# Early-fusion block on one core: the gated product of the expert layer goes from VectorE to ScalarE and GpSimd, and two expert units change stage

## The chip, the cores and the metric

The kernel runs on one core of a Trainium2 chip. A core has five engines that each run their own program: TensorE (PE in the profile, its weight loads PEld), VectorE (DVE), ScalarE (ACT), GpSimd (POOL) and SyncE (SP, which here issues the DMAs). They wait for each other only by semaphores. The metric is the device time of one execution in microseconds (us).

## The reference, cut to what matters

For each of 8 images an attention-free token mixer makes a hidden state `h` of 256 rows, 128 text embedding rows are put under it (T = 384 rows of 256), then comes attention with relative positions over 16 heads, then a dense mixture of 8 experts, which is where the change is:

```
weights = routing_weights(x, Wr, temperature)          # [T, 8], x = layernorm(h)
gate = einsum('btd,edi->beti', x, Wg)                  # all 8 experts, for all rows
up   = einsum('btd,edi->beti', x, Wu)
h    = silu(gate) * up                                 # the gated product
out  = einsum('bte,betd->btd', weights, einsum('beti,eid->betd', h, Wd))
```

## The kernel before, in words

**Rounds.** `rounds` (line 420) lays out one list of named steps per image and every engine walks the same list, doing its own part of each step (or nothing). Image `b` has the stages mix (`mix_in` to `project_v`), maxima (24 items), negate, attend (24 items) and out (`turn_outputs` to `rel_values`). The expert layer (FFN) of image `b-1` is cut into 48 units, and these are placed between the attention steps of image `b`. So there are 8 rounds with attention, of which 7 (b = 1 to 7) also carry the units of the image before, and a tail in which the last image's units run alone.

**Units.** Each expert `e` has two hidden tiles, n = 2e and 2e+1, of 128 hidden rows by T = 384 columns. `gate n` and `up n` are six fp32r matmuls each, into PSUM banks G and U (`hidden_tile`, matmul at L913). `down e 0` and `down e 1` are eight and four matmuls (L934). In the text g9 is gate 9, u9 up 9, d4.0 down 4 part 0. The order is g0 u0 g1 u1, then for each e: g(2e+2) u(2e+2) d(e).0 d(e).1 g(2e+3) u(2e+3).

**After each up.** ScalarE puts `silu(G)` into the single buffer `silu` (L1070); VectorE multiplies it with U into one of three slots of `hT` (L1362). A step after a unit is "late": `fill` holds it back and places it just ahead of the next unit, so behind every attention step that lies between. G may be written again when silu is done, U when the product is done (`h_done`), `silu` may be written again when the product is done; `down e 0` waits for the products of its two tiles. After each down VectorE adds the weighted result to `res` (L1374), which frees the PSUM banks D.

**Placement.** `FILL_MIX`, `FILL_MAXIMA`, `FILL_NEGATE` and `FILL_OUT` say how many units follow each step. Before: 26 units in mix, 8 in maxima (after items 2, 5, 8, ...), 3 in negate, 11 in out.

**Mix.** VectorE makes statistics of two tiles, GpSimd the root (L1405, L1408), VectorE normalises (L1115), GpSimd multiplies by `ln_g` (L1439) and adds `ln_b` (L1441), two tiles each; then statistics of three tiles, GpSimd's root again, VectorE's norm, and TensorE turns the result (L658, `turn_norm`) and projects. VectorE's routing steps lie in between. The projections q and k are each split in three bf16 parts (L1197, L1199, L1201), go through DRAM by SP's queue (L561, L566), and after them the relative logits come back as `band_t` (L595). ScalarE copies the logits out as bf16 at L1002.

**Maxima.** Item n is two score tiles in two of four banks. TensorE may write item n when VectorE has reduced item n-2 (L1220). The first item needs VectorE's copy of `band_t` (L1214). ScalarE re-orders further heads of the band (L1011). At item 13 `negate 0` turns the maxima found so far into bank 5, which is one of D's banks: TensorE first waits until VectorE has added the last down issued so far (`seen["down"]`).

**Out.** ScalarE copies the turned attention (L1047) and the turned weights (L1042); TensorE's `rel_values` (L874) and `residual` (L884) follow. SP writes and reads bands through DRAM (L631, L640).

Of the kernel before, what the change touches and what calls it, by code (L numbers as in the profile page):

```python
# [28 lines left out]
ALU = mybir.AluOpType  # L29
ACT = mybir.ActivationFunctionType  # L30
AX = mybir.AxisListType.X

P = 128
# [5 lines left out]
T = L + TXT  # L39
TT = T // P  # L40
IT = L // P
AH, AD = 16, 16
WIN = 4
NJ = 2 * WIN + 1
NE = 8
FI = 256
FT = FI // P
# [25 lines left out]
WINS = P // BL  # L73
# [6 lines left out]
FILL_MIX = [("residual", 0), ("mix_in", 0), ("turn_x2", 0), ("mix_sums", 0), ("router", 1),  # L80
            ("mix_out", 0), ("router_zone", 1), ("mix_norm", 1), ("router_rank", 2),
            ("norm_stats", 2), ("router_pick", 1), ("turn_norm", 2), ("project_qk", 0),
            ("project_rel", 1), ("project_v", 15)]
FILL_MAXIMA = [0, 0, 1] * 8
WEIGHTS_MAXIMA, WEIGHTS_ATTEND = (10, 18), (2, 12)
VALUE_TILES = (2, 0, 1)
FILL_NEGATE = 3
# [18 lines left out]
def fusion_block(nc, a, out):  # L106
    ctx = ExitStack()

    def sb(name, shape, dt=F32):
        return ctx.enter_context(nc.sbuf_tensor(name, shape, dt))  # L110
# [4 lines left out]
    def sem(name):  # L115
        return ctx.enter_context(nc.semaphore(name))

    def sig(name, n, unit=1, first=0):
        return Signal(sem(name), n, unit, first)

    with ctx:
# [24 lines left out]
        wu_hi = sb("wu_hi", [P, NE, KT, FI], F32R)  # L146
        wu_lo = sb("wu_lo", [P, NE, KT, FI], F32R)
# [19 lines left out]
        x2_hi = sb("x2_hi", [P, KT, T], F32R)  # L167
        x2_lo = sb("x2_lo", [P, KT, T], F32R)
        wgt = sb("wgt", [P, TT, NE])
        silu = sb("silu", [P, T])  # L170
        hT = sb("hT", [P, 3, T])
        stat = sb("stat", [P, TT, 6])
        mv = sb("mv", [P, TT, 2])
# [58 lines left out]
        O, G, U = S[:, 3], S[:, 6], S[:, 7]  # L232
# [56 lines left out]
        win_done = sig("win_done", WINS * AH // 2)  # L289
# [16 lines left out]
        R_STEPS = 24  # L306
        r_dve = sig("r_dve", R_STEPS)
        gate_pe, up_pe = sig("gate_pe", NE * FT), sig("up_pe", NE * FT)
        silu_done = sig("silu_done", NE * FT)
        h_done = sig("h_done", NE * FT)  # L310
        down_pe = sig("down_pe", 2 * NE)
        acc_done = sig("acc_done", NE * TT, first=1)
# [19 lines left out]
        def schedule(attention, ffn, more=True):  # L332
# [11 lines left out]
            def fill(n):  # L344
                for _ in range(min(n, len(left))):
                    unit = left.pop(0)
                    flush()
                    if owed and unit[0] == "down" and unit[2]:
                        steps.append(owed.pop())
                    steps.append(unit)  # L350
                    if unit[0] in after:
                        late.append((after[unit[0]],) + unit[1:])
                        seen[unit[0]] += 1
# [16 lines left out]
            for n in range(ITEMS):  # L370
                steps.append(("maxima", n))
                if not ffn and n in WEIGHTS_MAXIMA:
                    steps.append(("more_weights", WEIGHTS_MAXIMA.index(n)))
                fill(FILL_MAXIMA[n])
                if n == ITEMS // 2 + 1:
# [43 lines left out]
        def rounds(engine, parts):  # L419


            def do(step, b, f):
                part = parts.get(step[0])
                if part is not None:
                    part(f if step[0] in LATE_STEPS else b, *step[1:])

            for s in schedule(True, False):
                do(s, 0, None)
            with engine.Fori(1, NB - 1) as b:
                for s in schedule(True, True):  # L430
                    do(s, b, b - 1)
            for s in schedule(True, True, False):
                do(s, NB - 1, NB - 2)
            for s in schedule(False, True):
                do(s, None, NB - 1)
# [220 lines left out]
        def _(pe):  # L656
# [248 lines left out]
            def hidden_tile(f, n, dst, hi, lo, done, free):  # L905
                e, m = n // FT, n % FT

                if n:
                    pe.wait_ge(free.sem, free.at(f, n))
                j = 0  # L910
                for ws, xs in ((hi, x2_hi), (hi, x2_lo), (lo, x2_hi)):
                    for k in range(KT):
                        mm = pe.matmul(dst[:, 0:T], ws[:, e, k, m * P:(m + 1) * P], xs[:, k, :],  # L913
                                       start=(j == 0), stop=(j == 3 * KT - 1))
                        j += 1
                mm.then_inc(done.sem, 1)
# [2 lines left out]
                hidden_tile(f, n, G, wg_hi, wg_lo, gate_pe, silu_done)  # L919

            def up(f, n):
                hidden_tile(f, n, U, wu_hi, wu_lo, up_pe, h_done)

            def down(f, e, part):
                if part == 0:
# [6 lines left out]
                for i in ((0, 1), (2,))[part]:  # L932
                    for m in range(FT):
# [9 lines left out]
                        "turn_outputs": turn_outputs, "rel_values": rel_values, "turn_attn": turn_attn,  # L943
                        "residual": residual, "turn_x2": turn_x2, "router": router, "gate": gate,
                        "up": up, "down": down})


        @block.scalar
        def _(act):
# [116 lines left out]
            def gate(f, n):  # L1066
                act.wait_ge(gate_pe.sem, gate_pe.at(f, n + 1))
                if n:
                    act.wait_ge(h_done.sem, h_done.at(f, n))
                nc.scalar.activation(silu[:], G[:, 0:T], ACT.Silu).then_inc(silu_done.sem, 1)  # L1070

            rounds(act, {"mix_in": mix_in, "prepare": prepare, "turn_norm": turn_norm,
                         "project_qk": project_qk, "project_rel": project_rel, "maxima": maxima,
                         "negate": negate, "attend": attend, "copy": copy, "turn_weights": turn_weights,
                         "turn_attn": turn_attn, "turn_x2": turn_x2, "router": router, "gate": gate})


        @block.vector
        def _(dve):
# [131 lines left out]
            def maxima(b, n):  # L1211
                if n == 0:
                    dve.wait_ge(band_t_in.sem, band_t_in.at(b, 1))
                    dve.tensor_copy(band_h[:, :, 0:2], band_t[:, :, :, 0:2].rearrange("p i w h -> p i h w")  # L1214
                                    ).then_inc(band_first.sem, 1)
                dve.wait_ge(max_pe.sem, max_pe.at(b, n + 1))
                (h, i), (h2, _) = tiles_of(n)
                dst = maxima_sb[:, i, h:h + 2] if h2 > h else maxima_sb[:, 0:2, h]
                c0 = 2 * (n % 2)
                dve.tensor_reduce(dst, S[:, c0:c0 + 2, PAD:PAD + T], AX, ALU.max).then_inc(max_done.sem, 1)  # L1220
# [132 lines left out]
                step(dve.tensor_tensor(wgt[:], w, each(rt[8][:, :, 1]), ALU.mult))  # L1353
                assert k[0] == R_STEPS

            def hidden(f, n):
                dve.wait_ge(silu_done.sem, silu_done.at(f, n + 1))
                dve.wait_ge(up_pe.sem, up_pe.at(f, n + 1))
                if n >= 3:

                    dve.wait_ge(down_pe.sem, down_pe.at(f, 2 * ((n - 3) // FT + 1)))
                dve.tensor_tensor(hT[:, n % 3], silu[:], U[:, 0:T], ALU.mult).then_inc(h_done.sem, 1)  # L1362

            def accumulate(f, e, part):
                dve.wait_ge(down_pe.sem, down_pe.at(f, 2 * e + part + 1))
                if e and part == 0:
                    dve.wait_ge(acc_done.sem, acc_done.at(f, TT * e))
                last = e == NE - 1
                if last and part == 0 and not (isinstance(f, int) and f == NB - 1):

                    dve.wait_ge(win_done.sem, win_done.at(f + 1, WINS * 6))
                    dve.wait_ge(pv_done.sem, pv_done.at(f + 1, AH // GRP))
                for i in ((0, 1), (2,))[part]:
                    dve.scalar_tensor_tensor((out_st if last else res)[:, i], D[:, i // 2, (i % 2) * E:(i % 2 + 1) * E],  # L1374
                                             wgt[:, i, e:e + 1], res[:, i], ALU.mult, ALU.add
                                             ).then_inc(acc_done.sem, 1)
# [5 lines left out]
                         "turn_weights": turn_weights, "rel_values": rel_values, "residual": residual,  # L1382
                         "turn_x2": turn_x2, "router": router, "router_zone": router_zone,
                         "router_rank": router_rank, "router_pick": router_pick,
                         "hidden": hidden, "accumulate": accumulate})


        @block.gpsimd
        def _(pool):
# [12 lines left out]
            def root(b, stats, steps, done, tiles):  # L1402

                pool.wait_ge(stats.sem, stats.at(b, steps))
                nc.gpsimd.tensor_tensor(rstd[:, 0:tiles], mv[:, 0:tiles, 1], eps[:].broadcast_to([P, tiles]),  # L1405
                                        ALU.add).then_inc(done.sem, 1)
                pool.wait_ge(done.sem, done.at(b, 1))
                nc.gpsimd.tensor_tensor(rstd[:, 0:tiles], rstd[:, 0:tiles],  # L1408
                                        neg_half[:].broadcast_to([P, tiles]), ALU.pow
                                        ).then_inc(done.sem, 1)  # L1410
# [85 lines left out]
            def residual(b):  # L1496
                root(b, ln3, 2 * TT, ln3_root, TT)

            rounds(pool, {"mix_in": mix_in, "mix_sums": mix_sums, "mix_out": mix_out,
                          "mix_norm": mix_norm, "norm_stats": norm_stats, "project_rel": project_rel,  # L1500
                          "weights": weights, "attend": attend, "residual": residual})


# [36 lines left out]
```

## Time and profile before

| what | value |
|---|---|
| median of 3 runs | 1249.13 us (1246.06 to 1252.84) |
| profiled execution, own time | 1249.12 us |
| its span, first to last instruction | 1247.3 us, mean granted TensorE clock 0.952 |
| busy PE / DVE / ACT / POOL | 82% / 60% / 36% / 20% |

A timeline row gives the start, the length of the merged stretch, engine, line, operation, output and inputs, a count, and in square brackets how long the engine had been idle before it and what ended that. A stretch of x3 has three instructions. A row of groups gives the count, the busy time in us and the mean of one in ns, then the idle time before. A granted clock of 1.00 is 2.4 GHz and 0.50 is 1.2 GHz. A round is 143.37 us long in the middle of the run; the image-3 round's maxima stage starts at 518 us, and the image-4 round's mix stage lies about 595 to 661 us.

### The profile page before, as it was taken

What the parts mean: (1) busy time and instruction counts of PE and PEld (TensorE: products, weight loads), DVE (VectorE), ACT (ScalarE), POOL (GpSimd) and SP (SyncE); (2) the same over time, 40 slices, a digit from 0 to 9 for tenths busy, and PEclk for the clock granted to TensorE, in tenths of its full rate; (3) what the DMA queues carried; (4) which work ended last, traced back from release to release, by engine and by line L of the source; (5) the groups of instructions that cost most, each with busy time, mean ns of one, the idle gap of its engine ahead of it and who ended that gap; (6) DMA issues with size and microseconds to landing.
All of it is one profiled execution on the core that took longest, in us unless ns stands there. A gap on an engine that the chain in (4) does not pass through costs nothing.

```text
span 1247.3 us, 16776 instructions
## 1 busy us (share of the span) xinstructions
PE 1020.4 (82%) x5668; PEld 744.4 (60%) x5668; DVE 753.0 (60%) x1597; ACT 451.2 (36%) x651; POOL 247.8 (20%) x262
## 2 busy tenths in 40 slices
PE   3536698888898798888898798988988888987798
PEld 2412277636786287745786377854876367862687
DVE  7347355774648755685658745685567746487343
ACT  1133512453124723355124622346224531347211
POOL 6228411021200402013200412004120212004000
PEclk9569789989999999999999999999999999999899
DMA  4286203602062110802044020722026020620100
GB/s 110 101 240 174 68 5 97 140 11 53 4 178 59 24 42 33 202 10 39 18 121 115 9 56 0 202 44 39 18 79 157 10 52 5 179 60 18 35 1 13
DMA packets 96962, 87.87 MB, mean 70 GB/s; under 512 B 67281, under 2 KB 85074, under 8 KB 95090
## 3 DMA queue, kind: packets, MB, share of 16 engines
q1 hardware_dynamic: 96524, 86.24, 28.3%
q0 software_dynamic: 384, 1.05, 0.3%
q8 instruction: 17, 0.28, 0.1%
q14 instruction: 37, 0.30, 0.1%
HBM read 60.35 MB, written 26.92 MB: 70 GB/s over the span
## 4 chain that ended last, share of the span: by engine, by line
PE 46%; issue 22%; DVE 17%; DMA 5%; ACT 4%; POOL 4%; SPq 2%; POOLq 0%; DVEq 0%; ACTq 0%
PE S L913 16%; PE S L934 8%; DVE maxima L1220 4%; PE S L844 4%; PE S L779 4%; PE S L827 4%; PE S L741 3%; DVE S L1241 3%; ACT scratch L1033 3%; PE S L658 1%; DMA txt_row<-in_L_txt_W_E,txt_idx 1%; DVE res L1374 1%; PE S L760 1%; SPq L566 1%; PE S L787 1%
## 5 line engine op out<-in xcount | busy, mean ns | idle before, releaser
L1491 POOL TENSOR_TENSOR bands<-scratch,one 64x432 f32<-64x432 f32 x128 | 119.1, 931 | 525.0 <-ACT scratch L1033 519.4
L1070 ACT ACTIVATE silu<-S 128x384 f32<-128x384 f32 x128 | 63.0, 492 | 352.2 <-PE S L913 243.6
L1220 DVE TENSOR_REDUCE maxima<-S 128x2 f32<-128x768 f32 x192 | 172.2, 951 | 19.0 <-PE S L787 17.6
L934 PE MATMUL S<-w_d,hT 128*128 128x256 f32 x768 | 182.0, 382 | 1.5 <-DVE hT L1362 0.7
L1241 DVE TENSOR_TENSOR S<-S,bands 64x144 f32<-64x144 f32 x384 | 154.3, 402 | 43.3 <-PE S L827 32.6
L1033 ACT ACTIVATE scratch<-S 128x768 f32<-128x768 f32 x192 | 154.8, 812 | 56.3 <-DVE S L1241 43.0
L779 PE MATMUL S<-k_st,q_st 128*128 128x384 bf16 x384 | 101.9, 334 | 68.0 <-DVE maxima L1220 39.7
L934 PEld LDWEIGHTS S<-w_d,hT 128*128 128x128 f32 x768 | 143.4, 191 | 22.2 <-issue 2.3
L1362 DVE TENSOR_TENSOR hT<-silu,S 128x384 f32<-128x384 f32 x128 | 70.7, 552 | 116.7 <-PE S L913 97.4
L827 PE MATMUL S<-q_st,k_st 128*128 128x384 bf16 x384 | 98.8, 356 | 40.2 <-ACT scratch L1033 36.7
L1011 ACT ACTIVATE scratch<-scratch 128x816 bf16<-128x816 bf16 x56 | 92.3, 1694 | 41.5 <-DMA scratch<-d_band_t 41.5
L779 PEld LDWEIGHTS S<-k_st,q_st 128*128 128x128 bf16 x384 | 37.6, 98 | 116.3 <-DVE maxima L1220 58.0
L1374 DVE SCALAR_TENSOR_TENSOR res<-S,wgt,res 128x256 f32<-128x256 f32 x168 | 75.5, 479 | 48.0 <-PE S L934 47.7
L827 PEld LDWEIGHTS S<-q_st,k_st 128*128 128x128 bf16 x384 | 25.6, 99 | 132.1 <-ACT scratch L1033 104.0
L844 PE MATMUL S<-scratch,v_one 128*17 128x384 f32 x768 | 84.0, 522 | 12.4 <-ACT scratch L1033 12.3
L913 PE MATMUL S<-x_hi,wu_hi 128*128 128x384 f32 x256 | 72.1, 363 | 23.7 <-DVE hT L1362 23.7
L787 PE MATMUL S<-scratch,ident_b 128*128 128x132 bf16 (+1 forms) x384 | 85.7, 224 | 0.0
L913 PE MATMUL S<-x_hi,wg_hi 128*128 128x384 f32 x256 | 78.1, 386 | 0.0
L658 PE MATMUL S<-ident,scratch 128*128 128x128 f32 (+1 forms) x196 | 30.2, 294 | 51.5 <-DVE scratch L1115 29.9
L913 PE MATMUL S<-x_lo,wu_hi 128*128 128x384 f32 x256 | 66.4, 341 | 0.0
L913 PE MATMUL S<-x_hi,wg_lo 128*128 128x384 f32 x256 | 66.4, 341 | 0.0
L913 PE MATMUL S<-x_lo,wg_hi 128*128 128x384 f32 x256 | 66.3, 340 | 0.0
(167 smaller groups left out, 1515.6 us busy)
## 6 DMA issues: line engine op xcount, KB each, us to landing
bands<-d_band_s SPq DMA_DIRECT2D x16, 864.0 KB, 9.4
scratch<-d_band_t SPq DMA_DIRECT2D x8, 1632.0 KB, 9.6
d_parts<-scratch SPq DMA_DIRECT2D x48, 192.0 KB, 1.9
q_st<-d_parts SPq DMA_DIRECT2D x48, 192.0 KB
k_st<-d_parts SPq DMA_DIRECT2D x48, 192.0 KB
d_band_w<-bands SPq DMA_DIRECT2D x32, 240.0 KB, 3.9
out<-scratch SPq DMA_DIRECT2D x8, 384.0 KB, 2.6
x_in<-in_x SPq DMA_DIRECT2D x8, 256.0 KB, 3.6
```

Source lines behind the costliest of these rows:

```text
L779: pe.matmul(S[:, bank, PAD:PAD + T], q_st[:, h, i * P:(i + 1) * P], k_st[:, h, :], start=True, stop=False, skip_group_check=True)
L787: mm = pe.matmul(S[rows, bank, at + w0:at + w1], ident_b[rows, rows], band_h[rows, i, h, w0:w1], start=False, stop=True, skip_group_check= ...
L827: mm = pe.matmul(S[:, 2 * (n % 3) + l, PAD:PAD + T], k_st[:, h, i * P:(i + 1) * P], q_st[:, h, :], start=True, stop=True)
L844: mm = pe.matmul(S[32 * l:32 * l + VC, 6 + g % 2, 0:T], v_one[:, i, h, :], p_t[:, h % PTS, i, :], start=(i == VALUE_TILES[0]), stop=(i == ...
L913: mm = pe.matmul(dst[:, 0:T], ws[:, e, k, m * P:(m + 1) * P], xs[:, k, :], start=(j == 0), stop=(j == 3 * KT - 1))
L934: mm = pe.matmul(D[:, i // 2, (i % 2) * E:(i % 2 + 1) * E], hT[:, (FT * e + m) % 3, i * P:(i + 1) * P], w_d[:, e, m, :], start=(m == 0), s ...
L1011: nc.scalar.activation(band_h[:, :, heads], band_t[:, :, :, heads].rearrange("p i w h -> p i h w"), ACT.Copy).then_inc(band_turned.sem, 1)
L1033: nc.scalar.activation(dst, S[:, c0:c0 + 2, PAD:PAD + T], ACT.Exp).then_inc(exp_done.sem, 1)
L1220: dve.tensor_reduce(dst, S[:, c0:c0 + 2, PAD:PAD + T], AX, ALU.max).then_inc(max_done.sem, 1)
L1241: dve.tensor_tensor(win, win, band, ALU.add).then_inc(sc_add.sem, 1)
L1374: dve.scalar_tensor_tensor((out_st if last else res)[:, i], D[:, i // 2, (i % 2) * E:(i % 2 + 1) * E], wgt[:, i, e:e + 1], res[:, i], ALU. ...
L1491: nc.gpsimd.tensor_tensor(bands[rows, :, :, 2 * pair:2 * pair + 2].rearrange("p i w h -> p h i w"), win, one[rows].unsqueeze(2).unsqueeze( ...
```

## The change

The product leaves VectorE. ScalarE copies U into a new buffer `up_sb`; GpSimd multiplies `silu` by `up_sb` into `hT`. U is free after the copy (`up_copied`) and no longer after the product. `silu` and `up_sb` are single buffers, so silu n+1 and copy n+1 wait for product n on GpSimd. `project_v` is followed by 13 units for 15, and maxima has 10 units for 8: after items 1, 4, 5, 7, 10, 11, 13, 16, 17, 19. The units that change stage are d3.0 and d3.1, and every unit behind them up to u11 takes another place among the items.

```
-            ("project_rel", 1), ("project_v", 15)]
-FILL_MAXIMA = [0, 0, 1] * 8
+            ("project_rel", 1), ("project_v", 13)]
+FILL_MAXIMA = [0, 1, 0, 0, 1, 1] * 3 + [0, 1, 0, 0, 0, 0]
...
-        silu = sb("silu", [P, T])
+        silu, up_sb = sb("silu", [P, T]), sb("up_sb", [P, T])
...
             def up(f, n):
-                hidden_tile(f, n, U, wu_hi, wu_lo, up_pe, h_done)
+                hidden_tile(f, n, U, wu_hi, wu_lo, up_pe, up_copied)
...
+            def hidden(f, n):                       # ScalarE
+                act.wait_ge(up_pe.sem, up_pe.at(f, n + 1))
+                if n:
+                    act.wait_ge(h_done.sem, h_done.at(f, n))
+                nc.scalar.activation(up_sb[:], U[:, 0:T], ACT.Copy).then_inc(up_copied.sem, 1)
...
-            def hidden(f, n):                       # VectorE
-                dve.wait_ge(silu_done.sem, silu_done.at(f, n + 1))
-                dve.wait_ge(up_pe.sem, up_pe.at(f, n + 1))
-                if n >= 3:
-                    dve.wait_ge(down_pe.sem, down_pe.at(f, 2 * ((n - 3) // FT + 1)))
-                dve.tensor_tensor(hT[:, n % 3], silu[:], U[:, 0:T], ALU.mult).then_inc(h_done.sem, 1)
...
+            def turn_outputs(b):                    # GpSimd
+                pool.wait_ge(win_done.sem, win_done.at(b, WINS * AH // 2))
+
+            def hidden(f, n):                       # GpSimd
+                pool.wait_ge(silu_done.sem, silu_done.at(f, n + 1))
+                pool.wait_ge(up_copied.sem, up_copied.at(f, n + 1))
+                if n >= 3:
+                    pool.wait_ge(down_pe.sem, down_pe.at(f, 2 * ((n - 3) // FT + 1)))
+                nc.gpsimd.tensor_tensor(hT[:, n % 3], silu[:], up_sb[:], ALU.mult).then_inc(h_done.sem, 1)
```

## Rows read from the trace of the kernel before

**Rows 1.** The page: TensorE's busy time, and the ended-last chain by engine.

```profile
PE 1020.4 (82%) x5668; PEld 744.4 (60%) x5668; DVE 753.0 (60%) x1597; ACT 451.2 (36%) x651; POOL 247.8 (20%) x262
PE 46%; issue 22%; DVE 17%; DMA 5%; ACT 4%; POOL 4%; SPq 2%; POOLq 0%; DVEq 0%; ACTq 0%
```

**Rows 2.** Groups by line: busy us, mean ns of one, idle before.

```profile
L1362 DVE TENSOR_TENSOR hT<-silu,S 128x384 f32<-128x384 f32 x128 | 70.7, 552 | 116.7 <-PE S L913 97.4 <-ACT silu L1070 15.5 <-DVE scratch L1335 1.1
L1070 ACT ACTIVATE silu<-S 128x384 f32<-128x384 f32 x128 | 63.0, 492 | 352.2 <-PE S L913 243.6 <-DVE hT L1362 108.6
L1451 POOL TENSOR_TENSOR hid<-hid,bo_all 128x768 f32<-128x768 f32 x8 | 14.8, 1846 | 25.5 <-DVE scratch L1115 25.5
L1439 POOL TENSOR_TENSOR hid<-hid,ln_g 128x256 f32<-128x256 f32 x16 | 12.5, 784 | 7.0 <-DVE hid L1115 7.0
```

**Rows 3.** Timeline of the image-4 mix stage, by engine.

```profile
619.82 0.62 PE L913 MATMUL S<-x_hi,wu_hi 128*128 128x384 f32 x2 [1.54 <-DVE hT L1362]
621.53 0.73 POOL L1441 TENSOR_TENSOR hid<-hid,ln_b 128x256 f32<-128x256 f32 x1
623.67 0.62 PE L913 MATMUL S<-x_hi,wu_hi 128*128 128x384 f32 x2 [1.48 <-DVE hT L1362]
624.84 2.75 PE L934 MATMUL S<-w_d,hT 128*128 128x256 f32 x12
627.75 0.88 DVE L1374 SCALAR_TENSOR_TENSOR res<-S,wgt,res 128x256 f32<-128x256 f32 x2
629.64 0.87 PE L658 MATMUL S<-ident,scratch 128*128 128x128 f32 x6 [2.06 <-DVE scratch L1115]
```

**Rows 4.** Timeline of the image-3 round, end of mix and first maxima item.

```profile
496.49 0.56 ACT L1002 ACTIVATE scratch<-scratch 128x432 bf16<-128x432 f32 x1
497.62 0.96 DVE L1201 TENSOR_TENSOR scratch<-scratch 128x768 bf16<-128x768 f32 x1
514.04 2.75 PE L934 MATMUL S<-w_d,hT 128*128 128x256 f32 x12
516.78 1.67 ACT L1011 ACTIVATE scratch<-scratch 128x816 bf16<-128x816 bf16 x1 [3.10 <-DMA scratch<-d_band_t]
517.97 0.34 PE L779 MATMUL S<-k_st,q_st 128*128 128x384 bf16 x1 [1.18 <-DVE scratch L1214]
```

**Rows 5.** One line's instructions: shortest, median and longest ns.

```profile
L1332 DVE TENSOR_TENSOR scratch<-scratch,earlier x8: 358/784/787, 186.5 to 1187.5; 128x192 f32<-128x192 f32 x8
```

**Rows 6.** Image-3 maxima stage: timeline rows of PE and DVE.

```profile
519.64 0.34 PE L779 MATMUL S<-k_st,q_st 128*128 128x384 bf16 x1 [0.61 <-DVE maxima L1220]
520.06 0.59 PE L913 MATMUL S<-x_hi,wg_hi 128*128 128x384 f32 x2
521.20 0.34 PE L779 MATMUL S<-k_st,q_st 128*128 128x384 bf16 x1
525.08 2.69 DVE L1220 TENSOR_REDUCE maxima<-S 128x2 f32<-128x768 f32 x3 [0.54 <-PE S L787]
544.95 0.49 PE L658 MATMUL S<-ident,maxima 128*8 128x128 f32 x3 [0.19 <-DVE maxima L1220]
```

**Rows 7.** The same stage in the chain that ended last: start, us.

```profile
533.17 1.78 PE S L934 x8
```

**Rows 8.** Image-3 out stage, timeline of three engines.

```profile
589.17 0.86 ACT L1042 ACTIVATE scratch<-S 72x384 f32<-72x384 f32 x2 [0.89 <-PE S L658]
589.59 1.99 PE L934 MATMUL S<-w_d,hT 128*128 128x256 f32 x8
```

**Rows 9.** Window 1193 to 1197: length, busy us of PE, PEld, DVE, ACT, POOL, granted clock, DMA.

```profile
1193.00:1197.00 4.00, 4.00 (x16) 3.44 (x15) 1.08 (x3) 0.00 (x0) 0.00 (x0) 0.70 0.00 0
```

**Rows 10.** The tail's timeline, TensorE.

```profile
1191.78 0.82 PE L913 MATMUL S<-x_hi,wu_hi 128*128 128x384 f32 x2 [2.60 <-DVE hT L1362]
1193.68 3.62 PE L934 MATMUL S<-w_d,hT 128*128 128x256 f32 x12
1240.96 2.86 PE L934 MATMUL S<-w_d,hT 128*128 128x256 f32 x12 [0.70 <-DVE hT L1362]
```

More of the change, by code:

```diff
@@ L308, in fusion_block @@
         gate_pe, up_pe = sig("gate_pe", NE * FT), sig("up_pe", NE * FT)
-        silu_done = sig("silu_done", NE * FT)
+        silu_done, up_copied = sig("silu_done", NE * FT), sig("up_copied", NE * FT)
         h_done = sig("h_done", NE * FT)
@@ L1074, in _ @@
                          "negate": negate, "attend": attend, "copy": copy, "turn_weights": turn_weights,
-                         "turn_attn": turn_attn, "turn_x2": turn_x2, "router": router, "gate": gate})
+                         "turn_attn": turn_attn, "turn_x2": turn_x2, "router": router, "gate": gate, "hidden": hidden})
         @block.vector
@@ L1384, in _ @@
                          "router_rank": router_rank, "router_pick": router_pick,
-                         "hidden": hidden, "accumulate": accumulate})
+                         "accumulate": accumulate})
         @block.gpsimd
@@ L1497, in residual @@
                 root(b, ln3, 2 * TT, ln3_root, TT)
+            def turn_outputs(b):
[6 more added lines that the diff above has]
+                nc.gpsimd.tensor_tensor(hT[:, n % 3], silu[:], up_sb[:], ALU.mult).then_inc(h_done.sem, 1)
             rounds(pool, {"mix_in": mix_in, "mix_sums": mix_sums, "mix_out": mix_out,
                           "mix_norm": mix_norm, "norm_stats": norm_stats, "project_rel": project_rel,
-                          "weights": weights, "attend": attend, "residual": residual})
+                          "weights": weights, "attend": attend, "turn_outputs": turn_outputs, "residual": residual,
+                          "hidden": hidden})
 _NAMES = ["x", "L0_tok_w_bias", "L0_tok_Wk_b", "L0_tok_Wv_b", "L0_tok_Wq_b", "L0_tok_out_w", "L0_tok_out_b",
```

## The prediction, made before the changed kernel was run

> **What bounds the kernel now.** I read the page first. TensorE is busy 82% of the span and holds 46% of the chain that ended last, VectorE 17%, GpSimd 4% [rows 1]. So neither a lighter VectorE nor a heavier GpSimd says anything by its share; what counts is where TensorE waits. The groups by line say what the edit touches: 128 products of 552 ns on VectorE [rows 2]. The timelines then show where those lie. Where units follow each other TensorE never waits for a product. It waits in three places of each round:
>
> - Start of mix: 1.54 and 1.48 us for products, then 2.06 us for VectorE's norm, which comes behind the adds of d0.0 [rows 3].
> - End of mix: the twelve matmuls of d3.0 and d3.1, the two units that are to move, run from 514.04 to 516.79, and TensorE then waits 1.18 us for the band copy. ScalarE, which needs the same transfer, starts at 516.78 on the DMA itself [rows 4]. So the transfer ends this stage, not the units.
> - Maxima: VectorE's reductions (2.69 us for three, 0.87 us each to the next) are the clock of the stage, with a hole of 0.54 us for each gate or up put in [rows 6].
>
> **Durations of the new pieces.** Copy of U on ScalarE: like silu, also 128x384 out of PSUM, 0.49 us [rows 2]. Product on GpSimd: no row has its shape. 128x256 with two SBUF inputs takes 0.78 us, 128x768 takes 1.85 us [rows 2]; between them at the same slope it is 1.05 us. The bounds are those two rows; I take 1.05. A semaphore costs about 0.05 us between engines. So from the end of `up` to a usable product it is 0.49 + 1.05 + 0.1 = 1.64 us for 0.6 before.
>
> **Steady units (end of mix, tail): 0.** A pair of tiles takes TensorE 4.2 us. If u(2e+1) is readable at X, its product is there at X + 1.64, and d(e).0 is issued at X + 1.85 (the next gate and up, 2.11, less 0.26 of matmul drain). The cover is 0.2 us, so from a GpSimd product of about 1.25 us on each expert would stall. Silu of the next tile waits for the product and runs X + 1.6 to X + 2.1, again just in time. 63 us less on ScalarE's free time and 71 us less on VectorE buy nothing here.
>
> **Start of mix: +0.3 us a round.** By the order of steps product 0 stands on GpSimd behind the four `ln_g`/`ln_b` operations, which end at 622.26 [rows 3]. Product 0: 622.3 to 623.36. Silu 1 waits for it (single buffer): to 623.9. u1 runs early now (U is free after the copy: it need not wait until 619.82), but g2 waits for silu 1: 623.95. Then u2 at 625.0 and d0.0 at 626.05 (product 1 is ready at about 625.5). Its eight matmuls end at 627.83, the adds start at 628.03 where they started at 627.75 [rows 3], and norm and turn follow them. So the two old waits are gone (3.0 us) and in their place stands one wait of about 4.5 us, from 619.2 to 623.95. GpSimd's root for the next norm stands behind product 1, until 626.6, and is covered by the adds. Bounds: -0.5 (GpSimd quick) to +1.2 (product 1.85).
>
> **End of mix: +0.5 us a round.** Product 3 meets the split of k. Copy 3 comes behind L1002, which ends at 497.05, so the product wants to start at 497.6; VectorE's L1201, with both inputs in SBUF, starts at 497.62 [rows 4]. L1332 shows what such a meeting costs: 784 ns median where GpSimd works, 358 ns in the tail where it does not [rows 5]. If GpSimd is first, L1201, the DMAs queued behind it on SP (the last part, 12 stack transfers, `band_t`) and the end of the stage are 1.05 us later; if VectorE is first, nothing is lost. I take the middle, 0.5. The Trainium skill ("SBUF — State Buffer", "Who interferes with whom") says that a VectorE instruction with two SBUF inputs contends with a GpSimd instruction that reads SBUF, and that the one that issues second blocks until the first is done. The trace agrees for L1332; the rule speaks against this change, since the old product had one input in PSUM.
>
> Two units (1.78 + about 0.85 us) leave this stage, and that is worth 0, as the transfer ends it [rows 4]: TensorE only waits longer, 3.8 us for 1.2.
>
> **Maxima: +2.8 us a round.** I stepped the new order through with the row durations: item 0.42 us of issue (519.64 to 520.06), reducible 0.65 after its start; gate or up 1.14 us (520.06 to 521.20) [rows 6]; down 1.78 [rows 7] and 0.92; reduction 0.87 to the next and item n allowed after reduction n-2. For the old order this gives 26.75 us from item 0 to the last `negate`; the trace has 26.98 (517.97 to 544.95) [rows 4, 6]. For the new order it gives 29.55. VectorE's idle time inside grows from 2.1 to 5.0 us: 0.90 at d3.0 after item 1; 0.61 and 0.70 where g10 and u10 follow items 10 and 11 with no item between; and at d4.0 after item 13 0.47 waiting for the down and 1.21 for the turned maxima. The last is the change of order: `seen["down"]` is now 9, not 8, at `negate 0`, so the turn waits for the adds of d4.0 and VectorE for turn and ScalarE's copy. Its own work falls by only 0.1 (three products out, d3.0's adds in). Bounds: +1.5 (the negate pause half hidden) to +4.
>
> **Out: +2.3 us a round.** Product 15 is "late", so on ScalarE copy 15 stands behind `turn_weights`. Those two copies end at 590.03 [rows 8]. Copy 13 stood behind L1047 in the same way and held u14 by 0.2, so: 590.23, copy to 590.72, product to 591.82, and d7.0 at 591.87 instead of 589.59 [rows 8]. TensorE has nothing ahead of it, and all that follows to the next mix hangs on it. Bounds +1.5 and +3.1. If the copy stood ahead of `turn_weights` it would be 0.8.
>
> **Attend and negate: 0.** Copy 12 and product 12 end near 549.2, before GpSimd's first window.
>
> **TensorE's clock: +2.4 us a round.** In the tail TensorE waits 2.60 us until 1191.78 [rows 10]; the window 1193 to 1197 was granted 0.70, so part of it at the 1.2 GHz level [rows 9]. u2 took 1.90 us there and the twelve matmuls of d0 3.62 [rows 10], against 1.17 and 2.75 at 2.4 GHz [rows 3]: 1.6 us lost. The waits of 1.54, 1.48 and 2.06 us cost nothing. The change makes two waits over 2.6 us in each round, 4.5 at the start of mix and 3.8 before maxima, and what runs after each lies on the path (g2, u2, d0.0; items 0, 1 and d3.0). Bounds 0 and 1.6 each; I take 1.2, near the row, since the order leaves part of the slow stretch beside VectorE.
>
> **Tail: -3.0 us once.** Product 1 stood behind VectorE's routing; now u2 needs only copy 1, and g2, u2, d0 run on: -2.6 for the wait and -1.5 for its clock, together -4.1, of which 0.1 comes back as silu 1 waits for product 0: -4.0. At the end d7.0 waited 0.70 us [rows 10] and waits 1.04 more.
>
> **Sum.** 7 x (0.3 + 0.5 + 2.8 + 2.3) = 41.3; clock 7 x 2.4 = 16.8; tail -3.0: +55.1 on 1249.12 of the profiled execution, which is the median of the runs (1249.13). Forecast 1304.
>
> **Rivals.**
> - A, no clock falls. For it: waits up to 2.06 us cost nothing. Against: 2.60 did. 1249.1 + 41.3 - 3.0 = 1287.
> - B, the clock falls in two more places, at d7.0 (wait 2.3 to 2.4 us) and around `negate 0` (waits 1.1 and 1.4 us). 7 x 2 x 1.4 more: 1324.
> - C, only the maxima order costs; the waits at d7.0 and splits are covered by something I don't see. 7 x 2.8 - 3.0: 1266.
> - D, not slower: the end of mix hangs on TensorE's units after all. In rows 4 the band copy comes within 0.3 us of the last adds, so a transfer that has really landed by 514.2 would let the stage end 2.6 us sooner, and VectorE's 3 x 0.46 us of products would leave the norm chain too. 7 x -4.0 - 3.0: 1218. It decides only if the landing comes 2.6 us before ScalarE's start at 516.78, which ScalarE, idle for 3.10 us on that DMA, speaks against.
>
> **Chances.** Forecast 0.42, A 0.28, B 0.15, C 0.07, D 0.03, else 0.05. Range 1268 to 1326: from near C to just over B. A measurement of this kernel can tell about 0.5% from no change. Faster 0.04 (D and a bit), same 0.02, slower 0.94.
>
> **What would show it.** In the after trace: d7.0 with 2 to 2.5 us idle before it, released by GpSimd; g2 of mix waiting 4 to 5 us for silu; ScalarE's first L1011 again released by DMA, at the same distance from `turn_norm` or 1 us later with L1201 near 1.9 us; maxima 29 to 32 us long with a hole over 1 us before VectorE's `negate 0`; GpSimd's product 1.0 to 1.1 us; clock 0.5 after two waits. Wrong if: the product takes over 1.25 us (steady experts stall, some 8 x 8 times), or the stage starts sooner after the turn.

## The result, and the profile after

The changed kernel takes 1332.92 us (median of 4 runs, 1330.2 to 1335.99), the kernel before 1249.32 us: ratio 1.0662, 95% interval 1.0628 to 1.0696. The forecast was 1304 with a range to 1326. The direction was right; the loss is 84 us (81 between the two profiled executions) where 55 were forecast.

From the page of the changed kernel: busy time, chain by engine, and three groups. L1506 is the product on GpSimd, L1076 the copy on ScalarE.

```profile
PE 1060.1 (80%) x5668; PEld 776.8 (58%) x5668; DVE 698.5 (53%) x1469; ACT 507.0 (38%) x779; POOL 374.5 (28%) x390
PE 45%; issue 17%; DVE 12%; DMA 9%; POOL 5%; ACT 5%; SPq 5%; POOLq 0%; ACTq 0%; DVEq 0%
L1506 POOL TENSOR_TENSOR hT<-silu,up_sb 128x384 f32<-128x384 f32 x128 | 128.8, 1006 | 566.3 <-ACT up_sb L1076 539.0
L1070 ACT ACTIVATE silu<-S 128x384 f32<-128x384 f32 x128 | 62.9, 492 | 296.3 <-PE S L913 204.5
L1076 ACT ACTIVATE up_sb<-S 128x384 f32<-128x384 f32 x128 | 62.4, 488 | 66.3 <-PE S L913 66.3
```

The product takes 1.01 us (1.05 was taken), the copy 0.49. What does not fit is the first number: TensorE does the same 5668 matmuls and is busy 1060 us, for 1020 before [rows 1]. Work that was not added takes 40 us more, so the clock must be looked at. Its mean over the span is 0.919, for 0.952.

I then divided the round of image 4 by TensorE's first row of each stage, in both timelines (us):

| stage | before | after | added | forecast, without clock |
|---|---|---|---|---|
| mix_in to the turn (L658) | 32.18 | 35.15 | 2.97 | 0.3 |
| turn to first maxima item | 31.67 | 32.52 | 0.85 | 0.5 |
| maxima, to `negate 1` | 27.05 | 32.59 | 5.54 | 2.8 |
| `negate 1` to attend | 4.16 | 5.70 | 1.54 | 0 |
| attend | 27.73 | 27.86 | 0.13 | 0 |
| out, to `rel_values` (L874) | 14.57 | 16.97 | 2.40 | 2.3 |
| rest of the round | 6.04 | 6.05 | 0.01 | 0 |
| round | 143.40 | 156.84 | 13.44 | 5.9 |

Where the clock plays no part (out, turn to item) the terms hold to 0.1 and 0.35 us. Start of mix in the timeline of TensorE and GpSimd, to be held against [rows 3]:

```profile
652.09 1.11 POOL L1506 TENSOR_TENSOR hT<-silu,up_sb 128x384 f32<-128x384 f32 x1
653.84 1.01 PE L913 MATMUL S<-x_hi,wg_hi 128*128 128x384 f32 x2 [4.43 <-ACT silu L1070]
657.84 3.77 PE L934 MATMUL S<-w_d,hT 128*128 128x256 f32 x12
662.68 0.88 PE L658 MATMUL S<-ident,scratch 128*128 128x128 f32 x6 [1.07 <-DVE scratch L1121]
```

The two waits of 1.5 us are gone and one of 4.43 us stands in their place, as forecast. But d0's twelve matmuls then take 3.77 us, for 2.75. The maxima stage, TensorE and VectorE, against [rows 4, 6 and 7]:

```profile
695.20 0.50 PE L779 MATMUL S<-k_st,q_st 128*128 128x384 bf16 x1 [4.56 <-DVE scratch L1220]
696.89 3.72 PE L934 MATMUL S<-w_d,hT 128*128 128x256 f32 x8
701.27 2.69 DVE L1226 TENSOR_REDUCE maxima<-S 128x2 f32<-128x768 f32 x3 [3.17 <-PE S L787]
714.90 0.88 DVE L1372 SCALAR_TENSOR_TENSOR res<-S,wgt,res 128x256 f32<-128x256 f32 x2 [0.40 <-PE S L934]
715.83 0.49 PE L658 MATMUL S<-ident,maxima 128*8 128x128 f32 x3 [0.97 <-DVE res L1372]
716.96 0.55 DVE L1231 SCALAR_TENSOR_TENSOR neg_max<-S,neg_max 8x384 bf16<-8x384 f32 x1 [1.18 <-ACT neg_max L1020]
728.04 0.89 PE L913 MATMUL S<-x_hi,wg_hi 128*128 128x384 f32 x2
```

The first wait is 4.56 us (forecast 3.8 plus the split's delay). d3.0 takes 3.72 us for its eight matmuls, where d4.0 had 1.78 [rows 7], and VectorE's hole behind it is 3.17 us, not 0.90. VectorE's two pauses at `negate 0` are 0.40 us, for the down, and 1.18 us, for the turned maxima; 0.47 and 1.21 were worked out. TensorE's turn waits 0.97 us for the adds of d4.0. In the last row g12's first pair takes 0.89 us for 0.60: slow again, a third place. Windows over the three places give the granted clock; the columns are length, busy time and count of PE, PEld, DVE, ACT, POOL, then the clock:

```profile
653.50:660.00 6.50, 6.16 (x18) 5.75 (x19) 3.00 (x17) 1.65 (x4) 3.01 (x4) 0.51 0.00 0
695.00:701.00 6.00, 5.80 (x19) 4.01 (x20) 1.96 (x3) 2.64 (x3) 1.00 (x1) 0.51 0.53 115
728.00:732.00 4.00, 4.00 (x17) 3.96 (x15) 0.55 (x1) 1.00 (x3) 0.00 (x0) 0.57 0.02 6
```

These are 1.2 GHz for nearly all of 16.5 us. The round before had one slow stretch, 3.4 us within 697.0 to 700.6, some 4.5 us into attend; the changed kernel has that one too (738.2 to 741.8), so the three are new. The split of k, VectorE and GpSimd, against [rows 4]:

```profile
673.98 1.00 POOL L1506 TENSOR_TENSOR hT<-silu,up_sb 128x384 f32<-128x384 f32 x1 [9.41 <-ACT up_sb L1076]
674.04 1.75 DVE L1207 TENSOR_TENSOR scratch<-scratch 128x768 bf16<-128x768 f32 x1
```

GpSimd was first by 0.06 us and VectorE's step took 1.75 us, for 0.96; it is so in all seven rounds. The Trainium skill's rule ("SBUF — State Buffer", "Who interferes with whom") holds here: the later of the two is held up. The end of the out stage, against [rows 8]:

```profile
617.92 0.48 ACT L1076 ACTIVATE up_sb<-S 128x384 f32<-128x384 f32 x1
618.54 0.99 POOL L1506 TENSOR_TENSOR hT<-silu,up_sb 128x384 f32<-128x384 f32 x1 [4.67 <-ACT up_sb L1076]
619.66 1.99 PE L934 MATMUL S<-w_d,hT 128*128 128x256 f32 x8 [2.20 <-POOL hT L1506]
```

The tail from the turn (L658) to the end of the span is 68.6 us (1259.84 to 1328.4) for 71.8 before (1175.49 to 1247.3): -3.2, forecast -3.0. The last down waits 1.70 us, for 0.70 [rows 10]:

```profile
1322.04 2.86 PE L934 MATMUL S<-w_d,hT 128*128 128x256 f32 x12 [1.70 <-POOL hT L1506]
```

### The profile page after: what moved, and what is told of

It is laid out like the page before. It is cut to its first block, busy times and chain, and to the rows that moved or that the text cites. A ratio compares the mean times of both kernels' runs of the same rounds, so it can differ in the third digit from the quotient of the medians.

```text
span 1328.4 us, 17118 instructions
## 1 busy us (share of the span) xinstructions
PE 1060.1 (80%) x5668; PEld 776.8 (58%) x5668; DVE 698.5 (53%) x1469; ACT 507.0 (38%) x779; POOL 374.5 (28%) x390
## 3 DMA queue, kind: packets, MB, share of 16 engines
q0 software_dynamic: 384, 1.05, 0.3%
## 4 chain that ended last, share of the span: by engine, by line
PE 45%; issue 17%; DVE 12%; DMA 9%; POOL 5%; ACT 5%; SPq 5%; POOLq 0%; ACTq 0%; DVEq 0%
PE S L913 15%; PE S L934 10%; DMA scratch<-d_band_t 5%; PE S L844 4%; SPq L566 4%; PE S L779 4%; PE S L827 3%; DVE S L1247 3%; DVE maxima L1226 3%; PE S L741 3%; PE S L658 3%; ACT scratch L1033 2%; DMA txt_row<-in_L_txt_W_E,txt_idx 1%; PE S L787 1%; DVE scratch L1207 1%
## 5 line engine op out<-in xcount | busy, mean ns | idle before, releaser
L1506 POOL TENSOR_TENSOR hT<-silu,up_sb 128x384 f32<-128x384 f32 x128 | 128.8, 1006 | 566.3 <-ACT up_sb L1076 539.0
L934 PE MATMUL S<-w_d,hT 128*128 128x256 f32 x768 | 201.1, 410 | 17.0 <-POOL hT L1506 17.0
L934 PEld LDWEIGHTS S<-w_d,hT 128*128 128x128 f32 x768 | 154.0, 207 | 44.0 <-issue 15.8
L779 PE MATMUL S<-k_st,q_st 128*128 128x384 bf16 x384 | 108.9, 348 | 77.8 <-DVE scratch L1220 50.9
L913 PE MATMUL S<-x_hi,wg_hi 128*128 128x384 f32 x256 | 83.6, 410 | 31.2 <-ACT silu L1070 31.2
L1076 ACT ACTIVATE up_sb<-S 128x384 f32<-128x384 f32 x128 | 62.4, 488 | 66.3 <-PE S L913 66.3
L913 PE MATMUL S<-x_hi,wu_hi 128*128 128x384 f32 x256 | 75.2, 377 | 0.0
L913 PE MATMUL S<-x_lo,wg_hi 128*128 128x384 f32 x256 | 70.8, 360 | 0.0
L913 PE MATMUL S<-x_hi,wg_lo 128*128 128x384 f32 x256 | 70.7, 359 | 0.0
L913 PE MATMUL S<-x_lo,wu_hi 128*128 128x384 f32 x256 | 69.8, 355 | 0.0
```

The source lines that it names most:

```text
L779: pe.matmul(S[:, bank, PAD:PAD + T], q_st[:, h, i * P:(i + 1) * P], k_st[:, h, :], start=True, stop=False, skip_group_check=True)
L934: mm = pe.matmul(D[:, i // 2, (i % 2) * E:(i % 2 + 1) * E], hT[:, (FT * e + m) % 3, i * P:(i + 1) * P], w_d[:, e, m, :], start=(m == 0), s ...
L1506: nc.gpsimd.tensor_tensor(hT[:, n % 3], silu[:], up_sb[:], ALU.mult).then_inc(h_done.sem, 1)
```

## The experiments

The theory after the result (T): every term of the sum stands, except that the clock costs 2 to 3 times what was put down for it. The rival (N): the clock is a by-product, and the excess lies in the maxima order. Of each kernel the median and the ratio to the kernel before on the same chip are given. A difference in us to the change compares runs that were not made side by side; it is good to a few us.

**The two halves of the change apart.** `e1_engines` has the new engines with the old placement:

```diff
-            ("project_rel", 1), ("project_v", 13)]
-FILL_MAXIMA = [0, 1, 0, 0, 1, 1] * 3 + [0, 1, 0, 0, 0, 0]
+            ("project_rel", 1), ("project_v", 15)]
+FILL_MAXIMA = [0, 0, 1] * 8
```

> The engines of the change with the placement of units as before (15 after project_v, 8 in maxima). Theory T (the clock of TensorE falls after each wait of about 4 us, and each fall costs 2.7 us a round in mix and 2.7 in maxima; the rest as the prediction's terms): start of mix 0.3 + 2.7, the split of k 0.85, out 2.4, maxima 0, tail -3 once, so 7 x 6.25 - 3 = +41 on 1249, about 1290; the round's maxima stage stays 27.0 us. Rival N (the clock costs nothing, the excess over the prediction is in the maxima order): +22, about 1271.

`e2_order` has the same lines the other way round in the kernel before, product on VectorE.

> The placement of units of the change, with the product on VectorE as before. T: the end of mix has a wait of 3.7 us and a fall (2.7), maxima 3.0 by the row durations, a fall before attend 1.5 at most, start of mix and out unchanged: 7 x (5.7 to 7.2) = +40 to +50, about 1289 to 1299. N: only the 3.0, about 1270. If TensorE's moved units really shortened the end of mix, it would be near 1252.

Measured: `e1_engines` 1290.71 us, 1.036 (1.0327 to 1.0392); `e2_order` 1291.36 us, 1.0342 (1.0309 to 1.0376). Both totals are where T put them and 20 us from N. Neither half is the good one. The shares nearly add up: 3.6% + 3.4%, for 6.6% together. The total of `e1_engines` owes something to luck: maxima stays at 27.0 us in four of the seven rounds as T said, but the start of mix is +1.5 us in the image-4 round and from +1.5 to +3.0 over the seven, where T had +3.0 in all, and in three rounds the clock falls at d7.0, where T had no fall (out stage 18.0 to 18.3 us, for 16.97). In `e2_order` the stage from the turn to the first item keeps its length (31.52 us in the image-4 round, 31.67 before) though d3.0 and d3.1 have left it: the moved units were worth nothing there, since the transfer ends it, and rival D is out. TensorE's wait before the first item shows it, in its timeline:

```profile
678.56 0.50 PE L779 MATMUL S<-k_st,q_st 128*128 128x384 bf16 x1 [3.59 <-DVE scratch L1214]
```

3.59 us for 1.18 [rows 4], and the 0.50 us of this matmul (0.34 before) is the slow clock. Its maxima stage is 32.57 us, as in the full change.

**The clock by itself.** `e3_busy` is the changed kernel, and TensorE fills the two long waits with matmuls that nothing reads:

```diff
+            def keep_busy(count):
+                for _ in range(count):
+                    pe.matmul(S[:, 0, 0:T], wg_hi[:, 0, 0, 0:P], x2_hi[:, 0, :], start=True, stop=True)
...
             def gate(f, n):
+                if n == 2 and not (isinstance(f, int) and f == NB - 1):
+                    keep_busy(24)
...
                 if n == 0:
+                    if later(b):
+                        keep_busy(20)
                     pe.wait_ge(band_first.sem, band_first.at(b, 1))
```

> The changed kernel with idle time filled: 24 extra fp32r matmuls (4.2 us at 2.4 GHz) before gate 2 and 20 (3.5 us) before the first maxima item, in rounds 1 to 7, whose results nothing reads. T: the clock stays at 2.4 GHz in both places, 7 x 5.4 = 38 less than the change, about 1295, with the waits themselves as long as before. N: no gain, 1333, or more where the extra matmuls run past the wait.

Measured: 1294.31 us, 1.0381 (1.0356 to 1.0406), 39 us less than the change by the medians and 35 by the two ratios, for useless work added. Rows of TensorE at g2 in `e3_busy` (L909 are the added matmuls, L919 and L942 the gate and down), then two windows with the columns as above:

```profile
633.17 4.38 PE L909 MATMUL S<-x_hi,wg_hi 128*128 128x384 f32 x24
637.83 0.62 PE L919 MATMUL S<-x_hi,wg_hi 128*128 128x384 f32 x2 [0.28 <-ACT silu L1078]
640.05 2.75 PE L942 MATMUL S<-w_d,hT 128*128 128x256 f32 x12
643.88 0.88 PE L658 MATMUL S<-ident,scratch 128*128 128x128 f32 x6 [1.07 <-DVE scratch L1129]
```

```profile
632.00:646.00 14.00, 12.65 (x70) 11.67 (x69) 10.16 (x31) 2.88 (x7) 9.28 (x11) 1.00 0.00 0
676.00:700.00 24.00, 20.41 (x132) 15.08 (x133) 19.22 (x26) 11.48 (x13) 3.01 (x3) 1.00 0.38 76
```

The clock stays at 1.00 and g2 starts at the same distance after u1; d0 is back at 2.75 us. The stages become the forecast's: mix_in to the turn 32.58 us (+0.4; forecast +0.3), maxima 29.84 us (the stepping gave 29.55), `negate 1` to attend 4.17, so that the third fall went too although nothing was added there. N is out, and so is rival A, by which no clock falls. The Trainium skill ("TensorE: Matmul & The Clock Gate", "HAM oscillation — how this bites in real kernels") describes such a loop, in which a wait that returns in each turn makes each turn begin cold; `e3_busy` against the change agrees: the mean of the six middle rounds is 156.2 us in the change and 150.6 in `e3_busy`.

Not every fall went. In three of the seven rounds of `e3_busy` one lies at d7.0, behind the wait of 2.2 us that is followed by none in the other four. The image-4 round is one of them, and its out stage is 18.52 us, for 16.97:

```profile
753.51 3.54 PE L942 MATMUL S<-w_d,hT 128*128 128x256 f32 x8 [2.20 <-POOL hT L1514]
```

That is the first of the two places that rival B named.

**The single waits.** `e4_late` places the late product of the out stage early; `flush()` puts the steps that `fill` holds back into the list at once:

```diff
             for name, n in FILL_OUT:
+                if name in ("turn_attn", "turn_weights"):
+                    flush()
                 steps.append((name,))
```

> The changed kernel, with the late product placed ahead of turn_attn and turn_weights instead of behind them. T: copy 15 no longer stands behind the two copies of turn_weights on ScalarE, d7.0 waits 0.8 us or less instead of 2.2 to 2.4: 7 x 1.6 to 2.2 = 11 to 15 less, 1318 to 1322. Rival: product 15 is late because GpSimd is slow, not because of ScalarE's order: 1333.

Measured: 1321.4 us (1312.86 to 1330.04), 1.0574 (1.0512 to 1.0635). The down's wait fell from 2.20 to 1.13 us (0.8 or less was expected), the out stage from 16.97 to 15.57 us. In TensorE's timeline of `e4_late`:

```profile
621.87 1.99 PE L936 MATMUL S<-w_d,hT 128*128 128x256 f32 x8 [1.13 <-POOL hT L1508]
```

So ScalarE's order held it, and 1.0 us of copy and GpSimd is left. The profiled execution was the slowest of the four, at 1330 us: its start of mix is 1.6 us a round longer than in the change (36.75 us, 35.15), since the clock falls there already ahead of u0. The gain in the stage is sure. What reaches the total varies from run to run, and that the median meets the forecast is partly luck.

`e7_split` puts a `flush()` ahead of `project_qk` in the changed kernel, so that product 3 is done before the split of k.

> The changed kernel with product 3 placed ahead of project_qk. T: it no longer meets the last step of the split of k, which goes from 1.75 back to 0.96 us, and the band transfer lands 0.8 us earlier after the turn: 7 x 0.8 = 5 to 6 less than the change, 1327. Rival: the transfers are bound by their bytes and the landing does not move: 1333.

Measured: 1303.99 us, 1.0408 (1.0333 to 1.0483). The mechanism is there: L1209, the last step of the split, takes 0.96 us, and the turn to the first item 31.67 us, for 32.52. But 29 us were gained where 6 were expected. TensorE in `e7_split` at the two waits:

```profile
647.19 1.01 PE L915 MATMUL S<-x_hi,wg_hi 128*128 128x384 f32 x2 [4.43 <-ACT silu L1072]
650.71 2.75 PE L936 MATMUL S<-w_d,hT 128*128 128x256 f32 x12
686.20 0.34 PE L781 MATMUL S<-k_st,q_st 128*128 128x384 bf16 x1 [3.71 <-DVE scratch L1222]
```

The wait before maxima is 3.71 us, 0.85 less, and the item after it is fast (0.34). After the same 4.43 us in mix the slow stretch is over before d0. So the price of a wait is not fixed. With the wait before maxima 0.85 us shorter, the fall there is gone in four of the seven rounds, the one at `negate 1` in all seven, and the slow stretch in mix is half as long in five (33.64 us for 35.15 in the image-4 round). That the shorter wait did this, and not the shifted times of everything behind it, is not shown.

`e9_negate` moves d4.0 behind `negate 0` in the changed kernel:

```diff
-FILL_MAXIMA = [0, 1, 0, 0, 1, 1] * 3 + [0, 1, 0, 0, 0, 0]
+FILL_MAXIMA = [0, 1, 0, 0, 1, 1] * 2 + [0, 0, 1, 0, 1, 1] + [0, 1, 0, 0, 0, 0]
```

> The changed kernel with d4.0 after item 14 and not 13, so behind negate 0, which then waits for the adds of d3.1 only. By the row durations the maxima stage comes out at 27.9 us and not 29.6: 7 x 1.6 = 11 less, 1321 to 1322. Rival: the pause of negate 0 is hidden behind the reductions and nothing moves: 1333.

Measured: 1311.66 us, 1.0475 (1.04 to 1.0551). The maxima stage went from 32.59 to 30.89 us, -1.7 for the -1.6 stepped through; and `negate 1` to attend back from 5.70 to 4.17, which was not expected and makes it 21 us less for the 11 expected. So the third fall went with the pauses at `negate 0`, but they do not make it alone: in `e3_busy` and `e7_split` they stay (0.97 and 1.18 us) and the fall is gone.

**Can the new engines be had without the waits?** `e6_placed` has the new engines, the old placement of units, and a `flush()` ahead of `mix_norm`, `project_qk`, `turn_attn` and `turn_weights`.

> ScalarE's copy and GpSimd's product as in the change, the placement of units as before, and the late products placed ahead of mix_norm, project_qk, turn_attn and turn_weights instead of behind them. T (the engines' part of the loss is where the products stand in the order, and the clock that falls after the waits): product 0 fits before ln_g on GpSimd, so g2 waits 0.3 us, the turn comes 1 to 1.5 us earlier than before; no meeting with the split of k; out +1.0. 7 x (-1.3 + 0 + 1.0) - 3 = about 1244, same as before within 0.5%. Rival G (GpSimd is too slow for the product wherever it stands): it stays near e1_engines, 1275 to 1290.

Measured: 1261.01 us, 1.0051 (1.001 to 1.0092). The rival G (GpSimd is too slow wherever the product stands) is out, since 32 us of the 43 that `e1_engines` lost are gone; but my 1244 was missed. g2 waits 0.58 us, as meant; but product 1 now stands behind `ln_g` and `ln_b`, d0.0 waits 1.31 us for it, and the norm comes 2.79 us after the last unit:

```profile
623.94 0.62 PE L917 MATMUL S<-x_hi,wg_hi 128*128 128x384 f32 x2 [0.58 <-ACT silu L1074]
627.63 2.85 PE L938 MATMUL S<-w_d,hT 128*128 128x256 f32 x12 [1.31 <-POOL hT L1510]
633.28 1.36 PE L662 MATMUL S<-ident,scratch 128*128 128x128 f32 x6 [2.79 <-DVE scratch L1125]
```

The six turns of the last row take 1.36 us, for 0.87: the clock fell in that wait. The turn comes 0.4 us earlier than before, not 1.3: VectorE goes from its first norm (622.35) to the adds of d0.0 (631.38) with hardly a gap, and its ranking beside GpSimd is as slow as before. The rest of the loss is out, +1.0, and the clock: in the image-4 round the turn to the first item takes 33.25 us (31.67 before) and attend 29.02 (27.73), each with more time at the low clock.

**What bounds the start of mix.** The kernel before, product on VectorE. `e8_rank` and `e10_routing` only change the list of mix (shown against the old one):

```diff
-            ("mix_out", 0), ("router_zone", 1), ("mix_norm", 1), ("router_rank", 2),
-            ("norm_stats", 2), ("router_pick", 1), ("turn_norm", 2), ("project_qk", 0),
+            ("router_zone", 0), ("router_rank", 0), ("mix_out", 1), ("mix_norm", 3),             # e8_rank
+            ("norm_stats", 2), ("router_pick", 1), ("turn_norm", 2), ("project_qk", 0),
...
+            ("router_zone", 0), ("router_rank", 0), ("router_pick", 0), ("mix_out", 1), ("mix_norm", 3),  # e10_routing
+            ("norm_stats", 2), ("turn_norm", 3), ("project_qk", 0),
```

> The kernel before, product on VectorE, with router_zone and router_rank placed ahead of mix_out, where VectorE sits idle 4.3 us a round, so that the ranking stands neither in the norm chain nor beside GpSimd's ln_g and ln_b (0.78 us each there for 0.36 alone). Theory V (the start of mix is bound by VectorE's order, not by its load or by who makes the product): the turn comes 3 to 3.6 us earlier, 7 x 3 to 3.6 = 21 to 25 less than before, about 1225. Rival: GpSimd's roots and ln steps bound the norm chain as well and 1 us is left: 1242.

> The kernel before, product on VectorE, with all the routing steps (zone, rank, pick) ahead of mix_out and turn_norm ahead of d0.1, so that the norm no longer stands behind the adds of d0.0. V: the turn comes another 2 us earlier than in e8_rank (4 us earlier than before), TensorE waits about 1 us for it, and the clock does not fall there: 7 x 4 = 28 less than before, 1221 to 1226. Rival: the root on GpSimd ends later than the adds did and half of it stays, 1235.

Measured: `e8_rank` 1244.42 us, 0.9948 (0.992 to 0.9976); `e10_routing` 1232.68 us, 0.9879 (0.9853 to 0.9904). Both are faster than both kernels, with a quarter and a half of the gain that I expected. Both numbers lie nearer to the rivals' (1242 and 1235) than to mine. VectorE's ranking in `e8_rank` is back at its undisturbed length, 0.36 us for the 0.78 of [rows 5]:

```profile
607.26 0.36 DVE L1332 TENSOR_TENSOR scratch<-scratch,earlier 128x192 f32<-128x192 f32 x1
622.18 0.88 PE L658 MATMUL S<-ident,scratch 128*128 128x128 f32 x6 [2.02 <-DVE scratch L1115]
```

but the turn comes 1.8 us earlier (30.40 us after mix_in, 32.18 before) and not 3 to 3.6, because the pick and d0.0's adds still stand before the norm, and VectorE works through them without a gap. The rival is right in part: the statistics before them wait 0.24 us for GpSimd's `ln_b`. And after the 2.02 us wait in the last row the clock falls, so that the turn to the first item takes 33.21 us, for 31.67. That is so in three of the seven rounds; the other four have the same wait (2.02 to 2.05 us) and no fall there. `e10_routing` takes these out as well: 29.61 us, 2.6 us earlier than before. The 4 us of the expectation did not come: d0.1 now stands between the turn and the projections (32.54 us for 31.67), and TensorE waits 2.13 us for product 0, at u1. Product 0 stands behind VectorE's first norm, which waits 1.11 us for GpSimd's root, so the rival has a part here too. Behind that wait the matmuls run at the low clock in the image-4 round (first pair 1.01 us, 0.62 in [rows 3]). In four more rounds the clock falls within 2 us; in the two without a fall the turn comes after 28.95 us, for 29.61.

```profile
612.80 1.01 PE L913 MATMUL S<-x_hi,wu_hi 128*128 128x384 f32 x2 [2.13 <-DVE hT L1362]
```

**The best order with each engine.** `e11_both` is `e6_placed` with the list of `e10_routing`.

> The same order with ScalarE's copy and GpSimd's product, the products placed early as in e6_placed and the placement of units as before. V (the product's engine is worth nothing where it is placed well): the out stage keeps its 1.0 us a round, product 1 stands behind ln_g and ln_b and costs d0.0 another 0.5 to 1 us; 7 x 1.5 to 2 = 10 to 14 more than e10_routing. Rival (VectorE's relief of 0.55 us per product pays once the order is right): it is faster than e10_routing.

Measured: 1242.89 us, 0.9969 (0.9951 to 0.9987), 10.2 us more than `e10_routing` on the same chip, as expected. So with the same list the product is better kept on VectorE, though that engine is busy for 60% and the change takes 71 us of products from it. About 7 of the 10.2 us are the out stage (15.57 us for 14.57). `e10_routing` with its late products placed early was not run.

## Why the prediction was right in its steps and wrong in its size

- **What bounds the kernel** (TensorE's waits, not shares): right. VectorE is busy 54.5 us less, and that gave nothing.
- **Steady units, 0**: right. GpSimd's product is 1.01 us and no steady expert stalls; L934's waits for products are 17.0 us in 8, all at the stage places and the end.
- **Start of mix, +0.3**: right, once the clock is held (`e3_busy`: +0.4). The wait of "about 4.5 us" is 4.43.
- **End of mix, +0.5 and 0 for the moved units**: right. It was 0.85 in the image-4 round, GpSimd first; `e7_split` takes exactly that away. `e2_order` shows the 0.
- **Maxima, +2.8**: right, `e3_busy` has +2.8 (29.84). VectorE's pauses at `negate 0` are 0.40 and 1.18 us; `e9_negate` prices them at 1.7.
- **Out, +2.3**: right, 2.40; by `e4_late` 1.4 of it is ScalarE's order, and 1.0 is copy and product themselves.
- **Attend and negate, 0**: right for the work, wrong by 1.54 us for a clock fall at `negate 1`, which the sum did not have.
- **Tail, -3.0**: -3.2.
- **TensorE's clock, +2.4 a round**: this is the step that failed. Without clock the round was to grow by 5.9 us, and so it does: 0.4, 0.7 and 2.8 in `e3_busy`, and 2.4 for out in the change, where no clock falls in that stage, make 6.3. The clock took the rest in the image-4 round: start of mix 35.15 - 32.58 = 2.6, maxima 32.59 - 29.84 = 2.75, `negate 1` 1.5; together 6.9 us, where 2.4 were put down. I had priced a fall from the one in the tail (1.6 us after a wait of 2.60) and rounded it down to 1.2. After the waits of 4.43 and 4.56 us the stretch at 1.2 GHz was twice as long (6.8 us for 3.4). I took 1.6 for the upper bound, while the row was of a shorter wait, and gave further falls only to rival B, at 1.4 each, at d7.0 and around `negate 0`. In the change the third came at `negate 1`, in all seven rounds, and none at d7.0.
- **The sum**: the image-4 round taken for all seven gives 7 x (6.9 - 2.4) = 31 us more, so 1335 for the 1333 measured. That it fits so well is luck, since not every round has all the falls. Over the six middle rounds the mean length is 144.0 us before, 156.2 in the change and 150.6 in `e3_busy`. So filling the two waits takes away 5.6 us a round and leaves 6.6. By these, about 22 of the 29 us that the forecast missed are the clock (7 x 3.2) and about 5 the rest.

The range was too narrow for one reason: its upper end was rival B's 1324, and B too priced every fall, at 1.2 to 1.4 us, from a single row at a smaller wait than those the change makes.

## What to carry to other kernels

When a change puts a wait of several microseconds into a loop that TensorE runs, price the wait and then the work behind it at the 1.2 GHz level, and look for rows after waits of the same length; here the second was nearly as large as all other terms together. Moving an operation to an idle engine moves it into that engine's order: what counts is behind which steps it now stands. A copy added ahead of it stands in the order of a second engine (ScalarE's place alone made 1.1 us of the wait at d7.0, `e4_late`). A stage that a transfer ends gives nothing back for units taken out of it, while the stage that takes them in pays in full.

## What the runs showed of the hardware that was not expected

- The price of a wait is not a function of its length alone. 4.43 us in mix was followed by 6.8 us at 1.2 GHz in the change and by a stretch half as long in `e7_split`; 4.56 us before maxima was followed by 6.8 slow us, 3.71 us (`e7_split`) by none, 3.59 us (`e2_order`) by 6.8 again. The same wait differs from round to round too: 2.2 us at d7.0 has a fall in three of the seven rounds of `e3_busy` and none in the other four, 2.02 to 2.05 us before the turn likewise in `e8_rank`, and in the image-3 round of the change the first item after 4.32 us still runs at full speed (0.34 us in the row below), with 3.4 slow us only behind it. Small shifts elsewhere moved the total by 20 us and more (`e7_split` -29 for 6 expected, `e9_negate` -21 for 11). Why one falls and another doesn't was not settled.

```profile
539.62 0.34 PE L779 MATMUL S<-k_st,q_st 128*128 128x384 bf16 x1 [4.32 <-DVE scratch L1220]
```

- Adding 44 useless matmuls a round made the changed kernel 35 to 39 us faster (`e3_busy`).
- A VectorE and a GpSimd instruction that want to start within 0.06 us of each other: the one that came second took 1.75 us for 0.96.
